# Linear attention with two layer norms and an FFN on one core: where three sums, a score and some numerator copies stand in the hand-written order of the first stage

## The reference, cut to what matters

```python
q = q * cos + _rotate_half(q) * sin          # the same for k
qf = jax.nn.elu(q) + 1.0; kf = jax.nn.elu(k) + 1.0
def step(carry, inp):                        # over all 4096 positions
    state = state + k_s[..., :, None] * v_s[..., None, :]
    z = z + k_s
    num = jnp.einsum('bhe,bhed->bhd', q_s, state)
    den = jnp.einsum('bhe,bhe->bh', q_s, z)[..., None] + EPS
    return ((state, z), num / den)
...
x = _layernorm(x + attention(x)); x = _layernorm(x + ffn(x))
```

## Time and profile before

| | before |
|---|---|
| median of 3 runs | 2295.4 us (2294.45 to 2296.11) |
| profiled execution | 2293.33 us, span 2291.6 us, mean granted clock 0.997 |
| PE busy | 2252.7 us, 98% |
| DVE busy | 1827.2 us, 80% |
| ACT busy | 1276.8 us, 56% |
| POOL busy | 1128.0 us, 49% |

### The profile page before, as it was taken

The page is one execution under the profiler, slowest core; times in us unless marked ns, Lnnn a source line. Parts: engine busy times, 40 slices in busy tenths (PEclk is TensorE's granted clock), DMA queues, the critical chain, the costliest instruction groups (busy, mean ns, idle before and its releaser), DMA issues.

```text
span 2291.6 us, 32686 instructions
## 1 busy us (share of the span) xinstructions
PE 2252.7 (98%) x10226; PEld 1823.5 (80%) x10226; DVE 1827.2 (80%) x2479; ACT 1276.8 (56%) x2285; POOL 1128.0 (49%) x1007
## 2 busy tenths in 40 slices
PE   9899999999999999999999999999999999999998
PEld 7677878787878786788888778888888888888887
DVE  7877787868686868888888897787888788868877
ACT  7666666667676767243444555554445544554543
POOL 5766676767676867455544733322342133303321
PEclk9999999999999999999999999999999999999999
DMA  4111111102020115777778532323223322222323
GB/s 154 41 67 42 66 51 50 66 35 74 28 74 32 69 65 180 263 264 253 238 261 269 171 129 71 109 88 111 88 88 101 111 88 93 93 81 83 104 62 102
DMA packets 132710, 252.87 MB, mean 110 GB/s; under 512 B 44576, under 2 KB 45344, under 8 KB 122880
## 3 DMA queue, kind: packets, MB, share of 16 engines
q1 hardware_dynamic: 132608, 251.60, 33.0%
HBM read 188.11 MB, written 63.44 MB: 110 GB/s over the span
## 4 chain that ended last, share of the span: by engine, by line
PE 70%; issue 11%; POOL 10%; DVE 6%; ACT 2%; DMA 1%; POOLq 0%; SPq 0%; ACTq 0%; DVEq 0%
PE pj L626 16%; PE pj L709 11%; PE pnum L709 6%; PE pj L723 5%; PE psc L709 5%; PE pst L709 4%; PE psc L723 4%; PE pj L636 3%; PE pnum L723 3%; PE psc L657 3%; PE pnum L677 3%; PE pnum L680 3%; PE pst L723 2%; POOL fa L1415 1%; POOL fb L1416 1%
## 5 line engine op out<-in xcount | busy, mean ns | idle before, releaser
L1445 POOL TENSOR_TENSOR wcs<-wcr 128x256 f32<-128x256 f32 x64 | 67.8, 1060 | 514.6 <-DVE wcl L1187 506.0
L1482 POOL TENSOR_TENSOR tb<-tb,sinb 128x512 f32<-128x512 f32 x160 | 223.4, 1397 | 81.7 <-ACT tb L1007 81.5
L1485 POOL TENSOR_TENSOR Ql<-tb,Qh 128x512 fp32r<-128x512 f32 x128 | 172.5, 1350 | 64.1 <-ACT Qh L1016 64.1
L547 PE MATMUL pj<-woh,oh 128*128 128x512 f32 x512 | 201.7, 394 | 0.1
L626 PE MATMUL pj<-xah,wqh 128*128 128x512 f32 x500 | 198.8, 398 | 1.9 <-DVE Kf L1322 1.2
L547 PE MATMUL pj<-woh,ol 128*128 128x512 f32 x512 | 199.6, 390 | 0.0
L547 PE MATMUL pj<-wol,oh 128*128 128x512 f32 x512 | 199.3, 389 | 0.0
L626 PE MATMUL pj<-xal,wqh 128*128 128x512 f32 x500 | 195.5, 391 | 0.0
L626 PE MATMUL pj<-xah,wql 128*128 128x512 f32 x500 | 195.3, 391 | 0.0
L1310 DVE TENSOR_TENSOR pj<-pj,cosb 128x512 f32<-128x512 f32 x156 | 108.5, 696 | 71.9 <-ACT tb L1007 71.2
L709 PE MATMUL pj<-xch,wch 128*128 128x512 f32 x384 | 150.9, 393 | 5.8 <-DVE xcl L1193 3.7
(11 more groups left out here) (287 smaller groups left out, 7133.8 us busy)
## 6 DMA issues: line engine op xcount, KB each, us to landing
num_scratch<-no SPq DMA_DIRECT2D x128, 256.0 KB, 2.4
nt<-num_scratch SPq DMA_DIRECT2D x32, 1024.0 KB, 5.4
rb<-rden_scratch SPq DMA_DIRECT2D x32, 1024.0 KB, 6.4
wdr<-wd_scratch SPq DMA_DIRECT2D x128, 256.0 KB, 3.3
wcr<-in_wg SPq DMA_DIRECT2D x64, 256.0 KB, 2.8
wcr<-in_wu SPq DMA_DIRECT2D x64, 256.0 KB, 3.1
xst<-in_xT SPq DMA_DIRECT2D x34, 256.0 KB, 3.8
xr<-in_x SPq DMA_DIRECT2D x32, 256.0 KB, 5.6
```

The source lines that it names most:

```text
L547: last = nc.tensor.matmul(py[s][:, :], a[s][:, h, :], b[:, h, :], start=(h == 0 and i == 0), stop=(h == H - 1 and i == 2))
L1482: nc.gpsimd.tensor_tensor(tb[c][:, :], tb[c][:, :], sinb[:, :], ALU.mult).then_inc(sin_done, 1)
L1485: nc.gpsimd.tensor_tensor(Ql[g % 2][:, c, :], (tb[c] if c else Kf)[:, :], f32(Qh[g % 2][:, c, :]), ALU.subtract).then_inc(lo_done, 1)
```

## The change

Only the tables change, not what is computed. On TensorE `D1` moves ahead of `U11`, `C23` ahead of `U21` and `D3` ahead of `U33`. On ScalarE `O10` moves ahead of `N12` and `A12`, `O20` ahead of `A22`, `O21` ahead of `A23`, and in the start block `O01` ahead of `N03`. Vector, GpSimd and SyncE keep their order.

```diff
 ORDER_PE = """
-J21 U03 C11 C12 Z10 J22 J23 J24 Z11 U10 C13 U11 D1 J30 Z12 J31 C20 U12 Z13 C21 T2 U13 J32 J33 Z20 J34 Z21 C22
-U20 U21 C23 D2 Z22 U22 J00' Z23 T3 U23 C30 J01' Z30 C31 C32 J02' J03' U30 J04' Z31 U31 V0' Z32 J10' Z33 C33 V1'
-C00' T0' C01' U32 U33 D3 J11' J12' Z00' U00' J13' Z01' J14' U01' V2' V3' C02' C03' Z02' J20' D0' Z03' T1' U02'
+J21 U03 C11 C12 Z10 J22 J23 J24 Z11 U10 C13 D1 U11 J30 Z12 J31 C20 U12 Z13 C21 T2 U13 J32 J33 Z20 J34 Z21 C22
+U20 C23 U21 D2 Z22 U22 J00' Z23 T3 U23 C30 J01' Z30 C31 C32 J02' J03' U30 J04' Z31 U31 V0' Z32 J10' Z33 C33 V1'
+C00' T0' C01' U32 D3 U33 J11' J12' Z00' U00' J13' Z01' J14' U01' V2' V3' C02' C03' Z02' J20' D0' Z03' T1' U02'
 C10'
 """
```

The last tile's `LAST_PE` has the first two of these, not the third. One line of ScalarE's table and the one of the start block:

```diff
-A20 N20 O12 K2 X31 A21 O13 L30 L31 S32 S33 N21 X32 H0' S34 H1' A22 N22 H2' O20 X33 L32 H3' A23 X34 L33 N23 O21
+A20 N20 O12 K2 X31 A21 O13 L30 L31 S32 S33 N21 X32 H0' S34 H1' O20 A22 N22 H2' X33 L32 H3' O21 A23 X34 L33 N23
-w16 A03 X14 N03 L14 S20 O01 w17 w18 K1 N10
+w16 A03 X14 O01 N03 L14 S20 w17 w18 K1 N10
```

More of the change, by code:

```diff
@@ L51 @@
 ORDER_ACT = """
-O02 A10 X20 S21 O03 L20 A11 N11 X21 L21 S22 S23 X22 S24 L22 X23 N12 A12 O10 L23 X24 A13 O11 L24 S30 N13 S31 X30
-A20 N20 O12 K2 X31 A21 O13 L30 L31 S32 S33 N21 X32 H0' S34 H1' A22 N22 H2' O20 X33 L32 H3' A23 X34 L33 N23 O21
+O02 A10 X20 S21 O03 L20 A11 N11 X21 L21 S22 S23 X22 S24 L22 X23 O10 N12 A12 L23 X24 A13 O11 L24 S30 N13 S31 X30
+A20 N20 O12 K2 X31 A21 O13 L30 L31 S32 S33 N21 X32 H0' S34 H1' O20 A22 N22 H2' X33 L32 H3' O21 A23 X34 L33 N23
 O22 L34 S00' K3 N30 O23 A30 X00' S01' A31 N31 L00' X01' S02' L01' S03' A32 X02' O30 L02' S04' X03' N32 O31 L03'
@@ L184 @@
 LAST_PE = """
-J21 U03 C11 C12 Z10 J22 J23 J24 Z11 U10 C13 U11 D1 J30 Z12 J31 C20 U12 Z13 C21 T2 U13 J32 J33 Z20 J34 Z21 C22
-U20 U21 C23 D2 Z22 U22 Z23 T3 U23 C30 Z30 C31 C32 U30 Z31 U31 Z32 C33 U32 Z33 U33 D3
+J21 U03 C11 C12 Z10 J22 J23 J24 Z11 U10 C13 D1 U11 J30 Z12 J31 C20 U12 Z13 C21 T2 U13 J32 J33 Z20 J34 Z21 C22
+U20 C23 U21 D2 Z22 U22 Z23 T3 U23 C30 Z30 C31 C32 U30 Z31 U31 Z32 C33 U32 Z33 U33 D3
 """
```

## The result

The changed kernel takes 2298.31 us (median of 20 runs, 2296.17 to 2302.29), the kernel before 2294.27 us in the same comparison (20 runs). The ratio is 1.0019, 95% interval 1.0013 to 1.0026: 4.4 us slower, between 3.0 and 6.0. Forecast were +4.9 us and 2300.3 us. Of the 2.0 us between 2300.3 and 2298.31, 1.1 us lie in the base: the forecast started from the median of three runs, 2295.4 us. The slowdown is clear of no change, but whether it is over 0.2%, which the forecast gave 0.55, the interval leaves open.

What follows compares the result with a forecast made beforehand. TensorE was taken as the bound, so only its waits could move the time. The terms 5.25 − 0.48 + 0.1 gave +4.9 us on the 2295.4 us median, so 2300.3 us, range 2295.0 to 2303.0.

Steps and rivals of the forecast that it cites:

- The PE order costs nothing by itself: On TensorE, moving each `D` or `C` past a `U` changes neighbours but adds no work: cost 0.
- U33 ends 1.20 later, and the group behind A01' with it: ScalarE's `A01'` waits for `U33`; it and the queued ScalarE, Vector and GpSimd instructions, up to `I11'`, move by 1.20 us.
- The scan falls behind I12': Vector's scan `Q1'` is held up by GpSimd's `I12'`, now first, and ends at 389.00, 1.60 us later than before.
- the rival's 0.35: Vector's scan is not blocked, `N01'` moves by 1.20 alone: 0.30 + 0.05 us a tile; chance 0.11.
- the sign "a scan of over 2 us": Sign that the forecast is right: `I12'` runs before Vector's scan, and the scan takes over 2 us.
- the first of its rivals: Vector's scan gets through before or beside `I12'`: +2.5 us, with the other terms +2.1, time 2297.6 us; chance 0.11.
- the second: Rival: no wait at `Z01'` at all, only the start term is left, time 2295.0 us; chance 0.11.
- 0.75 us a tile, seven tiles: TensorE's `Z01'` starts 0.70 us late and the matmul behind it adds 0.05: +5.25 us over seven tiles.
- The ScalarE copies: In the loop the early `O20` gains 0, its store being held in the SP queue; the later `A22` is hidden.
- the margin of 0.2 us at `A22`: Vector's `H10'` hides ScalarE's later `A22` with 0.2 us to spare; otherwise up to 0.48 us a tile at `U22`.
- The start block: `O01` moves into idle time ahead of the weight piece, so the first tile's `J21` starts earlier: −0.48 us.
- The last tile: No `H10'` hides the later `A22` there; about 0.3 of slack out of 0.48: +0.1 us (between 0 and 0.48).

Runs made afterwards that it cites:

- The experiment with `S12'`: The changed kernel with ScalarE's `S12'` moved behind `X11'` and `N01'`; ratio 1.0014 (1.0005 to 1.0023) against the kernel before.
- the version with the store ahead: The changed kernel with `D3` back behind `U33` and SyncE's store of `O20` ahead of `B1'` and the cosine/sine loads; ratio 0.9993 against the kernel before.

## Why the prediction was right

**The PE order costs nothing by itself: right but for 0.06 us.** In the rows above `D30` takes 1.00 with its neighbours moved, and the version without the third edit has tiles of the old lengths. With `D3` ahead of `U33`, the second matmul of `J11'` starts at 380.44 instead of 380.38 (379.77 + 0.61), so 0.06 us a tile are the new order's own.

**U33 ends 1.20 later, and the group behind A01' with it: right, 1.26 measured.** The sum had 1.19 to 1.20; the missing hundredths are later matmuls of `U33` that start 0.24 and not 0.23 apart.

**The scan falls behind I12': right.** The forecast had `P04'` end at 386.81, the scan end at 389.00 and `N01'` at 389.99 in the time of before. With 0.61 added these are 387.42, 389.61 and 390.60; measured are 387.43 (385.65 + 1.78), 389.66 (387.95 + 1.71) and 390.64. The experiment with `S12'` shows that the block is a cause of its own, with 0.40 of the 0.73 us. The prediction had given the block 0.40 too (0.75 against the rival's 0.35). Two slips in its text don't touch the sum: the sign "a scan of over 2 us" doesn't follow from its own times, which give 389.00 − 387.33 = 1.67; and a shared bandwidth without a full block would be the first of its rivals, not the second. That Vector and GpSimd exclude each other while such an instruction runs is the rule of the Trainium skill, SBUF — State Buffer, section SBUF: two separate sides; the runs agree, with a scan of 1.27 us when it starts first and of 1.71 us when it asks 0.63 us before GpSimd's instruction ends. If nothing of the scan went on during the block, it would be 0.63 + 1.27 = 1.90 us, so some 0.2 us of it aren't held up.

**0.75 us a tile, seven tiles: right.** 5.27 us over the seven tiles of the changed kernel, against 5.25. In the version with this edit alone 0.73 and 0.71 us a tile, and 5.0 us by its ratio.

**The ScalarE copies: right in the loop.** The store left the queue at 340.97, 44.27 us after the tile's start, as before (340.37 − 296.09 = 44.28), and `O22` still waited for it. Moving the store does what moving the copy couldn't. Whether the margin of 0.2 us at `A22` held: Vector's `A22` started when `H10'` let it, and `U22` was no later.

The renamed wait is worth a look. GpSimd's `G22` and TensorE's `U22` in the changed kernel, tile 3:

```profile
340.81 0.63 POOL L1492 TENSOR_SCALAR_AFFINE_SELECT Al<-Al 128x512 fp32r<-128x512 f32 x1
```

```profile
341.59 0.47 PE L677 MATMUL pnum<-Ah,Vh 128*128 128x512 f32 x1 [0.62 <-ACT no L1045]
```

`U22` starts 0.15 after `G22` has ended at 341.44; before it was 0.14. But it waits for two semaphores, the masked scores' and the copies'. The count of the second had been reached with `O20` long before; `O21`, now early, ends at 341.46 and raises the same semaphore once more, and the list names whoever raised one last. The wait is `G22`'s. Of the version that keeps the copies late and moves only `D3` the list still says `Al`, 6.9 us in 10. One tile settles it. Where `H3'` waited for its load in the version with the store ahead, `O21` came late, and ended only after `U22` had started:

```profile
562.12 0.58 ACT L1045 ACTIVATE no<-pnum 128x512 f32<-128x512 f32 x1
```

```profile
562.34 0.47 PE L677 MATMUL pnum<-Ah,Vh 128*128 128x512 f32 x1 [0.62 <-POOL Al L1492]
```

The wait is as long, 0.62 us, and has its old name.

**The start block: the term that failed.** The prediction took Vector's weight piece and `Y0` to move with ScalarE's, and `J21` to start 0.48 earlier. The matmul ahead of it started 1.38 us before it in the kernel before and 1.32 after. Vector's weight piece and `Y0` in the changed kernel, then in the kernel before, and GpSimd's instruction of that stretch in the changed one:

```profile
65.38 1.75 DVE L1296 TENSOR_TENSOR wql<-rq,wqh 128x512 fp32r<-128x512 f32 x1 [1.78 <-ACT wqh L992]
67.05 0.68 DVE L1361 COPY dn<-pj 128x512 f32<-128x512 f32 x1
```

```profile
66.20 1.27 DVE L1296 TENSOR_TENSOR wql<-rq,wqh 128x512 fp32r<-128x512 f32 x1 [2.27 <-ACT wqh L992]
67.39 0.68 DVE L1361 COPY dn<-pj 128x512 f32<-128x512 f32 x1
```

```profile
65.30 1.28 POOL L1482 TENSOR_TENSOR tb<-tb,sinb 128x512 f32<-128x512 f32 x1
```

The piece did start 0.48 earlier against the rest, and then took 0.48 longer: it ran into GpSimd's instruction from 65.30 to 66.58 and ended 0.55 us after it, as before. In all six versions with `O01` early the piece takes 1.74 or 1.75 us, in the three without 1.26 or 1.27. The step followed ScalarE and Vector and left GpSimd out, where a few lines above the same pair had been followed. It is 0.06 us instead of 0.48. With it the sum would have been +5.3, and the measured +4.4 lies 0.9 below; its interval reaches 6.0. That +4.9 came nearer than +5.3 is luck.

**The last tile: +0.1, not contradicted.** `Z23` starts 46.90 us after that tile's start instead of 46.80; in the other four versions with the early copies it is 46.84 to 46.87, in the other three with late ones 46.80 to 46.82. The tile's own length is no measure: it is 67.7 to 67.9 us in four of the nine profiles and 69.3 to 69.4 in the other five, with and without these edits; what decides that wasn't tried.

## What to carry to other kernels

An instruction that moves on a saturated engine can cost next to nothing there and still cost time, by the end of the one that it displaces: look up who waits for that one, and what is queued behind the waiter. Where two engines exclude each other, a delay of one can change who goes first, and then it grows: here the scan took 0.44 us longer. A delay of 1.2 us met 0.9 us of slack, and more than half of the loss came from the exchange and not from the delay. A copy made early is worth nothing while its store stands in an ordered queue behind other loads, and a wait for several semaphores is named after the one raised last, so a renamed row needn't be a new wait.

## What the runs showed that I had not expected

That the same exclusion swallows an earlier start entirely (0.48 us in the start block), and that whether the `C30` wait appears differs from tile to tile and from profile to profile with the landing of one store: it stands in five of the seven tiles before, in six after, in three with `D3`'s move alone, in two without it and in two with `S12'` behind, and in none once the store is ahead. The versions with two or three ran on one chip; each has one profile only, so whether the chip decides isn't shown. This alone moves a run by up to 0.6 us a tile, and it is most of what the tiles' lengths differ by in one profile.
